# A four-layer graph attention network on one core: a relu moved into VectorE's scaling, and every engine's operations in a new order

## What is computed

```python
h = jnp.maximum(_layernorm(x, axis=-1), 0.0)          # before each of the four layers
# layer 0: one head, weights W only enter the scores; elu after it
# layer 1: a layer of 4 heads (512 -> 1024), elu, then a layer of one head (1024 -> 512)
# layer 2: one head, mask with self loops
# layer 3: 8 heads of 64 features:
xh  = (x @ W_proj) split in 8 heads
scores = leaky_relu(a_src[i] + a_dst[j] + b_att, 0.2), masked where A == 0
att = softmax(scores, axis=-1)
out = relu(att @ xh)
```

## Time and profile before

| | |
|---|---|
| median of three runs | 3287.21 us |
| the profiled execution's own time | 3295.56 us |
| its span (first to last instruction) | 3293.5 us |
| PE busy | 3084.6 us (94%), in 21776 matmuls |
| ACT busy | 2494.8 us (76%) |
| DVE busy | 2268.0 us (69%) |
| POOL busy | 2104.4 us (64%) |
| mean granted TensorE clock | 0.976 of 2.4 GHz; 1.00 in all slices but the first two and the last |

### The profile page before, as it was taken

The page is one execution under the profiler, slowest core; times in us unless marked ns, Lnnn a source line. Parts: engine busy times, 40 slices in busy tenths (PEclk is TensorE's granted clock), DMA queues, the critical chain, the costliest instruction groups (busy, mean ns, idle before and its releaser), DMA issues.

```text
span 3293.5 us, 77652 instructions
## 1 busy us (share of the span) xinstructions
PE 3084.6 (94%) x21776; PEld 2800.7 (85%) x21776; DVE 2268.0 (69%) x5867; ACT 2494.8 (76%) x6689; POOL 2104.4 (64%) x3236
## 2 busy tenths in 40 slices
PE   1689999999999999999999999999999999999974
PEld 0579899998989999898999989899998989999863
DVE  6467777777777777777777777777777777777652
ACT  2358788887888888788878878888887888788763
POOL 4246666666667666666666666666766666666643
PEclk6799999999999999999999999999999999999996
DMA  4012222212222222222222222222222122222211
GB/s 136 27 45 61 72 65 65 72 61 77 61 72 65 64 73 61 77 61 72 65 62 75 61 76 61 71 66 60 76 61 76 61 69 68 60 77 61 64 39 43
DMA packets 170069, 217.14 MB, mean 66 GB/s; under 512 B 34864, under 2 KB 100528, under 8 KB 169648
## 3 DMA queue, kind: packets, MB, share of 16 engines
q1 hardware_dynamic: 169648, 212.18, 21.5%
HBM read 177.55 MB, written 34.54 MB: 64 GB/s over the span
## 4 chain that ended last, share of the span: by engine, by line
POOL 40%; issue 36%; ACT 13%; PE 4%; DVE 3%; POOLq 1%; ACTq 0%; DVEq 0%
POOL rs L1386 8%; ACT eE L940 8%; POOL rs L1389 5%; POOL g_lo L1458 5%; POOL eE L1470 5%; POOL eE L1477 4%; POOL rs L1384 3%; POOL e_L L1422 3%; ACT eB L863 3%; DVE nmE L1295 3%; POOL eB L1451 3%; POOL e_L1b L1422 2%; POOL mask_loop L1416 1%; PE bank_b L365 1%; ACT hT_hi L921 1%
## 5 line engine op out<-in xcount | busy, mean ns | idle before, releaser
L1495 POOL TENSOR_TENSOR out_sb<-rE,x 128x512 f32<-128x512 f32 x128 | 165.4, 1293 | 541.9 <-ACT rE L981 541.9
L365 PE MATMUL bank_b<-w_hi,hT_hi 128*128 128x344 f32 x1536 | 473.4, 362 | 11.8 <-DVE hT_lo L1221 10.0
L365 PE MATMUL bank_c<-w_hi,g_hi 128*128 128x258 f32 x2048 | 412.4, 283 | 1.1 <-DVE x L1177 1.1
L365 PE MATMUL bank_c<-w_lo,g_hi 128*128 128x258 f32 x2048 | 413.4, 283 | 0.0
L365 PE MATMUL bank_b<-w_lo,hT_hi 128*128 128x344 f32 x1536 | 412.5, 323 | 0.0
L940 ACT ACTIVATE eE<-eE,st 128x128 f32<-128x128 f32 x1024 | 326.2, 390 | 55.2 <-POOL eE L1470 55.2
L1470 POOL TENSOR_TENSOR eE<-t_all_L,mask 128x512 f32<-128x512 f32 x256 | 352.9, 1379 | 21.2 <-DMA t_all_L<-t_dram_L 21.2
L365 PE MATMUL bank_c<-w_hi,g_lo 128*128 128x258 f32 x2048 | 361.6, 289 | 0.8 <-DVE g_lo L1264 0.5
L365 PE MATMUL bank_b<-w_hi,hT_lo 128*128 128x344 f32 x1536 | 359.1, 328 | 0.0
L365 PEld LDWEIGHTS bank_b<-w_hi,hT_hi 128*128 128x128 f32 x1536 | 280.0, 190 | 90.1 <-issue 68.2
L365 PE MATMUL bank_e<-w_hi,hT_hi 128*128 128x264 f32 x1024 | 336.6, 344 | 5.8 <-DVE rE L1319 5.8
(11 more groups left out here) (137 smaller groups left out, 8836.0 us busy)
## 6 DMA issues: line engine op xcount, KB each, us to landing
t_all_L<-t_dram_L SPq DMA_DIRECT2D x128, 512.0 KB, 4.2
x_in<-in_x SPq DMA_DIRECT2D x128, 256.0 KB, 2.5
t_all_L1a<-t_dram_L1a SPq DMA_DIRECT2D x128, 256.0 KB, 4.3
out<-out_sb SPq DMA_DIRECT2D x128, 256.0 KB, 4.5
t_all_L<-t_dram_L SPq DMA_DIRECT2D x256, 64.0 KB, 2.9
adj_in<-in_adj SPq DMA_DIRECT2D x128, 64.0 KB, 2.5
t_dram_L1a<-t_rows_L1a SPq DMA_DIRECT2D x512, 0.5 KB
t_all_L1b<-t_dram_L1b SPq DMA_DIRECT2D x128, 64.0 KB, 2.8
```

Source lines behind the costliest of these rows:

```text
L365: last = mm(bank[:, 0:width], a[:, c * P:(c + 1) * P], w[:, c, b * width:(b + 1) * width], start=(first and c == chunks[0] and n == 0), st ...
L1495: tt(out_sb[:, g.slot(OR), :], rE[:], x3[:, g.slot(X3R), :], ALU.add).then_inc(sem("out_made"), 1)
```

## The change

`relu_L3` goes from ACT. DVE's `result_L3` becomes two instructions, one for each half of the heads, that take the maximum with zero and multiply by the reciprocal; POOL's `out_L3` waits for them directly. All lists get a new order, and most operations work on a graph one turn later (SKEW 12 for 10); turns outside the stretch `t.full` carry more waits, and the waits of the operations that share a bank of PSUM are adapted to the new order.

```diff
-SKEW = 10
+SKEW = 12
...
-                        pe.wait_ge(sem("x1_made"), g.made(-1))
+                        pe.wait_ge(sem("x1_made"), g.made())
...
-            def relu_L3(g):
-                if g.live:
-                    act.wait_ge(sem("out_read"), g.made())
-                    activation(rE[:], rE[:], ACT.Relu).then_inc(sem("rE_relu"), 1)
...
-                    rc4 = rcE[:].rearrange("p b (k a) -> p b k a", a=1).to_broadcast([P, 2, HB, K3])
-                    tt(r4, wide[:, :, :, 0:K3], rc4, ALU.mult).then_inc(sem("out_read"), 1)
+                    rc4 = rcE[:].rearrange("p b (k a) -> p b k a", a=1)
+                    for i in range(2):
+                        last = stt(r4[:, i], wide[:, i, :, 0:K3], 0.0,
+                                   rc4[:, i].to_broadcast([P, HB, K3]), ALU.max, ALU.mult)
+                    last.then_inc(sem("out_read"), 1)
...
-                    pool.wait_ge(sem("rE_relu"), g.made())
+                    pool.wait_ge(sem("out_read"), g.made())
...
-                load(t.graph(0))
...
+                load(t.graph(1))
...
-                product_L2(t, t.graph(7))
-                project_L3_first(t, t.graph(9))
-                turn_exp_L1b(t, t.graph(5))
-                product_L0(t, t.graph(2))
-                product_L1b(t, t.graph(5))
-                project_L1a_high(t, t.graph(3))
+                project_L1a_last(t, t.graph(4))
+                product_L1a_first(t, t.graph(5))
+                product_L2(t, t.graph(8))
+                turn_exp_L1b(t, t.graph(6))
+                project_L3_first(t, t.graph(10))
+                turn_exp_L0(t, t.graph(3))
```

More of the change, by code:

```diff
@@ L748, in _ @@
-                turn_exp_L1b(t, t.graph(5))
-                product_L0(t, t.graph(2))
-                product_L1b(t, t.graph(5))
-                project_L1a_high(t, t.graph(3))
+                product_L1b(t, t.graph(7))
+                product_L0(t, t.graph(4))
+                project_L1a_high(t, t.graph(5))
+                project_L1a_low(t, t.graph(5))
+                project_L1b_first_high(t, t.graph(6))
+                turn_h3(t, t.graph(10))
+                project_L1b_first_low(t, t.graph(6))
@@ new lines, in _ @@
+                project_L1b_last(t, t.graph(6))
+                turn_exp_L3_last(t, t.graph(11))
+                turn_exp_L3_first(t, t.graph(11))
+                turn_prob_L1a(t, t.graph(5))
+                product_L3_last(t, t.graph(11))
+                product_L3_first(t, t.graph(11))
+                product_L1a_last(t, t.graph(5))
+                turn_h1(t, t.graph(4))
+                turn_mask(t, t.graph(4))
+                project_L3_last_high(t, t.graph(10))
+                project_L3_last_low(t, t.graph(10))
@@ L1012, in _ @@
[L1012 to L1016, removed]
+                pT_L0(t.graph(4))
+                g_hi_last(t.graph(6))
+                g_hi_first(t.graph(6))
+                norm_0(t.graph(3))
+                norm_3(t.graph(10))
+                values_L3(t.graph(11))
+                leaky_L3_last(t.graph(11))
+                leaky_L3_first(t.graph(11))
@@ L1018, in _ @@
+                elu_last(t.graph(5))
+                leaky_L0(t.graph(3))
+                leaky_L1b(t.graph(6))
+                pT_L2(t.graph(8))
+                exp_L0(t.graph(3))
+                exp_L1b(t.graph(6))
+                elu_first(t.graph(5))
+                pT_L1b(t.graph(6))
+                norm_2(t.graph(7))
         @block.vector
@@ L1324, in _ @@
                 make_rows(t)
[L1325 to L1336, removed]
@@ L1350, in _ @@
[L1350 to L1362, removed]
+                rows_L2(t.graph(8))
@@ new lines, in _ @@
+                sources_L3(t.graph(11))
+                residual_L0(t.graph(4))
+                columns_L0(t.graph(3))
+                values_L1a(t.graph(5))
+                moments_0(t.graph(2))
+                g_lo_first(t.graph(6))
+                rows_L0(t.graph(3))
+                most_L3_last(t.graph(11))
+                most_L1a(t.graph(5))
+                most_L3_first(t.graph(11))
+                hT_lo_L3(t.graph(10))
+                stats_1(t.graph(4))
+                recip_L1a(t.graph(5))
```

179 lines of the change are left out of this document (80 added, 99 removed).

## The result

The kernel takes 3216.93 us (median of 4 runs, 3215.49 to 3219.2), the kernel before 3287.22 (4 runs): a ratio of 0.9779, 95% interval 0.9767 to 0.9791 (the two medians alone give 0.9786). That is 70 us less where 22 were forecast. The profiled execution took 3215.87 us, its span is 3213.9, that of before 3293.5: 79.6 less.

What follows compares the result with a forecast made beforehand. PE's work bounds the kernel, 23.36 of 24.04 us a turn; with 0.5 waited for g_lo a turn takes 23.86, 0.18 less, times 119 is 21 us, 22 with the relu: 3287.2 − 22 = 3265, range 3202 to 3294.

Steps and rivals of the forecast that it cites:

- PE's own work: PE, busy 2773 of 2810 us in the middle, sets the time; its work alone is 23.36 of 24.04 us a turn.
- the wait for pE: PE's idle before L3's transposes of ACT's exponential pE, 0.47 a turn at its start; the new order should end it.
- the loop to pE: Late product, elu, g_hi, g_lo, scale_3, masks, leaky, exponentials, PE again; the new order takes 1.9 us of POOL out.
- The relu: relu_L3 moved from ACT to DVE: worth nothing in the middle, 0.6 us once in the last turn; cost 0 to 0.05.
- The taking of turns: DVE and POOL instructions that both read two SBUF tensors go one after the other, alternating; 50 in 100, likeliest 3265.
- mask 5.25 to 6.4, column 1 to 7.0, mask to 8.2, column 2 to 8.85: POOL's masks alternate with DVE's columns_L0, in us after product_L2's start; values_L1a then starts at 8.9 instead of 8.34.
- the 0.5 of waiting: PE wants DVE's half of g_lo at 10.45, it is ready at 11.0: 0.5 us waited a turn.
- lock without effect: Rival: columns_L0 is through before the masks, or the instructions overlap; 23.4 a turn, 76 us gained, 3210; 21 in 100.
- slower: Rival: DVE gets its turn later, the wait for g_lo passes 0.68; 3301 or some 3395; 17 in 100.
- No effect: Rival: pE wait stays because the loop runs through ACT, leaky_L1a or L1a's exponential 0.9 later; 24.04, 3286; 12 in 100.

Runs made afterwards that it cites:

- the swap undone: Kernel after with the halves of product_L1a (with their g_hi and elu) back in the old order, first early, last late: 3243.68 us, ratio 0.9849.
- The controls: Kernel after plus a third instruction in columns_L0: with two SBUF inputs 3392.3 us, ratio 1.0297; with one (BN_STATS of h) 3219.18 us, ratio 0.9777.

## Why the prediction was right in sign and wrong in size

**Right.** PE's own work is the bound and takes 23.36 a turn (23.35 measured in turns without a wait). What was to be won was waiting. The new order took the wait for pE away. With scale_3's place, the order of masks and leaky relus, or the swap undone, a wait comes back, worth 0.60, 0.46 and 0.25 a turn (72, 54 and 30 us over 119 turns); they don't add up (1.31 against the 0.57 won). Only the second of them is a wait for pE. Undoing scale_3's place or the swap brings a wait for g_lo, so that these two broke the loop to pE, as the prediction has it, is not shown for the new order; moving scale_3 alone did end that wait in the old one. The relu is worth nothing. The taking of turns of two-input DVE instructions and POOL's happens in nearly all turns, in the forecast sequence. The Trainium skill (SBUF — State Buffer, section Who interferes with whom) states that a VectorE instruction with two SBUF inputs contends with a GpSimd instruction that reads SBUF, and one with at most one does not. The controls agree: 1649 ns against 684. It also calls the conflict an exclusive lock; by the listed durations the two don't exclude each other wholly, since a mask of 1.17 and a column of 0.68 take 1.57 in turn.

**Wrong.** The step that failed is the term "mask 5.25 to 6.4, column 1 to 7.0, mask to 8.2, column 2 to 8.85", and with it the 0.5 of waiting. Measured: mask from 5.09, column 1 to 6.74, column 2 to 8.31. Three parts:

- The masks start 0.16 earlier. The forecast had them wait for the table; POOL's g_lo ends later than that and sets their start.
- A mask and a column in turn take 1.57 together (6.74 to 8.31), and 1.65 the first time, where 1.85 and 1.75 were laid out. The forecast summed 1.15 to 1.2 for a mask, the duration listed for one, and 0.6 to 0.65 for a column; but listed durations of neighbours on one engine overlap too (0.61 from start to start where 0.68 is listed). Even the unhindered distances of starts, 1.12 and 0.61, sum to 0.15 more than was measured, so instructions of the two engines must overlap by that much; how was not looked into. The other traces have the same distance: 1.58 from the second column to values_L1a in the kernel with the halves as before (1184.45 to 1186.03). 0.28 + 0.10 = 0.38 less.
- The forecast put 0.05 between the second column and values_L1a; there is none. So it starts at 8.31 instead of 8.90, which is just when the L1a projection lets it start (8.31 as well in the turn of 1201.17, where DVE was idle for 0.62 ahead of it).

Unhindered columns would end 1.22 after their start, at 6.64, and DVE would have nothing to do for 1.67. The taking of turns fills this gap to the last hundredth, and costs nothing there. What it leaves is that POOL's `make_mask` comes to stand beside g_lo.

So a turn is 23.36 + 0.1 (0.07 where g_lo takes 0.78 beside `make_mask`, which the forecast did not lay out, and some late turns) instead of 23.36 + 0.5: 119 × 0.39 = 47 us, the whole distance of the forecast from the measured median (3265 − 3217 = 48). The rival "lock without effect" had the time (3210), and of its two reasons the second in part: not that the columns go first, but that instructions overlap.

The rival "slower" described another kernel: L1a's mask that "holds up g_lo itself (11.1)" is what the order with scale_3 back does (10.98 in most turns, 11.08 in the one shown), and the new kernel avoids. "No effect" fell: PE is at pE at 14.26 and doesn't wait for it.

**Open.** The filling's 4 us; why of two turns with the same listed starts one gives the column the first go, and of two others `make_mask` or g_lo; and what the other changes of the order (PE's list, ACT's copy of the mask, the later turns of most operations) are worth, which no run took apart.

## What to carry to other kernels

A contended instruction cost here only what reached past the next fixed start on its engine. Lay out the room first and compare to hundredths: masks that started 0.3 us later made most turns 0.3 longer. Don't sum a chain by listed durations; take distances of starts, and where two engines contend, take them from a place where they already do (1.57 here, against 1.85 by durations). Lay out what follows the contended stretch too: here `make_mask` beside g_lo, 0.07 a turn. When several small edits of an order each seem worth a share of a wait, undo them one by one: here each alone brought back 44 to 105% of the 0.57 a turn, and not always as the same wait.

## What the runs showed of the hardware that was not expected

- DVE instructions with two inputs from SBUF and POOL's additions, both 512 columns, alternate one by one in the turns shown, with a period of 1.57 to 1.58 us, though alone they follow each other at 0.61 and some 1.12 us: in all 0.15 less than the two in a row.
- The same pair of listed starts (0.02 apart) went both ways in one trace; the price was 1.70 against 0.68 for DVE.
- A POOL instruction with one tensor input contends too: `make_mask` (128x128) and DVE's g_lo, 0.04 to 0.06 us apart, take 0.30 and 0.78 or 0.86 and 0.65.
- An instruction of the same length with one input (BN_STATS of h) was not held up at all: 684 ns beside the masks, 688 elsewhere.
